# Rounding without relying on the integer cast, in a transformer layer's quantized feed-forward

## The reference, cut to what matters

```
def _quant_weight(w):
    s = jnp.clip(jnp.mean(jnp.abs(w)), EPS, None)
    wq = jnp.clip(jnp.round(w / s), -1.0, 1.0) * s
    ...
def _quant_act(x):
    scale = 127.0 / jnp.clip(jnp.max(jnp.abs(x), axis=-1, keepdims=True), EPS, None)
    xq = jnp.clip(jnp.round(x * scale), -128.0, 127.0) / scale
    ...
def _bitlinear(x, w):
    return jnp.einsum('bsi,oi->bso', _quant_act(x), _quant_weight(w))
...
x = x + attention(layernorm(x))
h = gelu(_bitlinear(layernorm(x), w1))      # 4096 wide
x = x + _bitlinear(h, w2)
```

## Time and profile before

| what | us |
|---|---|
| median of 3 runs | 8665.15 (8665.02 to 8674.39) |
| the profiled execution, timed as the runs are | 8699.92 |
| its span, slowest core | 8698.4 (8636.6 to 8698.4 over the cores) |
| TensorE busy | 4222.9 |
| VectorE busy | 2331.2 |
| ScalarE busy | 1927.1 |

### The profile page before, as it was taken

One profiled execution on the slowest core, in us unless ns is written; L12 is line 12 of the kernel. 1 busy time (PEld: TensorE's weight loads), 2 busy tenths in 40 slices (PEclk: granted clock), 3 DMA queues, 4 the chain that ended last, 5 costly groups with the idle time before them and its releaser, 6 DMA issues.

```text
span 8698.4 us, 58407 instructions; the slowest of 8 cores (8636.6 to 8698.4 us)
## 1 busy us (share of the span) xinstructions
PE 4222.9 (49%) x19456; PEld 1649.1 (19%) x19456; DVE 2331.2 (27%) x4241; ACT 1927.1 (22%) x2129; POOL 0.2 (0%) x4
## 2 busy tenths in 40 slices
PE   4224555666666536546666664203334433035545
PEld 0000211222222212112222222101112211012222
DVE  0431323111111122331111111465444444730000
ACT  1012211444443222014444342111000011001111
POOL 0000000000000000000000000000000000000000
PEclk8666665555555556555555555556666666568778
DMA  4242100000000110000000001111122211221221
GB/s 165 92 135 89 32 0 0 1 1 1 1 1 1 37 63 18 0 0 1 1 1 1 1 1 41 61 44 49 61 85 72 73 58 58 73 85 44 73 78 56
DMA packets 199057, 358.61 MB, mean 41 GB/s; under 512 B 23257, under 2 KB 154718, under 8 KB 194674
## 3 DMA queue, kind: packets, MB, share of 16 engines
q1 hardware_dynamic: 198770, 354.87, 12.6%
HBM read 279.29 MB, written 75.50 MB: 41 GB/s over the span
## 4 chain that ended last, share of the span: by engine, by line
PE 43%; DVE 24%; ACT 15%; issue 8%; DMA 6%; SPq 3%; DVEq 1%; ACTq 0%
ACT pslab L763 7%; PE ps_PV L773 6%; PE ps_S L752 6%; PE ps_F L1182 6%; PE ps_F L1068 5%; PE pss L265 4%; PE ps_qn L730 3%; PE ps_W L830 2%; PE ps_mu L606 2%; DVE colmisc L1099 2%; DVE ao_tm L785 2%; PE ps_rs L610 2%; PE ps_proj L485 2%; PE ps_trH L1121 2%; DMA f2xst<-scr_x 2%
## 5 line engine op out<-in xcount | busy, mean ns | idle before, releaser
L752 PE MATMUL ps_S<-qt,kt 65*128 65x512 bf16 x2048 | 985.1, 611 | 278.9 <-ACT pslab L763 242.6
L763 ACT ACTIVATE pslab<-ps_S 128x1024 bf16<-128x1024 f32 x1024 | 994.6, 1021 | 152.3 <-PE ps_S L752 150.4
L1182 PE MATMUL ps_F<-hqin,w2tb 128*128 128x512 bf16 x2048 | 493.5, 403 | 541.1 <-DMA f2xst<-scr_x 408.9
L773 PE MATMUL ps_PV<-vaug,pslab 128*128 128x65 bf16 x8192 | 531.5, 242 | 457.2 <-DVE ao_tm L785 369.5
L783 DVE RECIPROCAL colmisc<-ps_PV 128x1 f32<-128x1 f32 x512 | 86.1, 168 | 1950.9 <-PE ps_PV L773 1950.9
L773 PEld LDWEIGHTS ps_PV<-vaug,pslab 128*128 128x128 bf16 x8192 | 463.2, 129 | 573.0 <-issue 573.0
L265 PE MATMUL pss<-wab,s_onescolf 128*1 128x512 f32 x512 | 309.4, 755 | 518.9 <-ACT wab L245 306.1
L1068 PE MATMUL ps_F<-w1tb,yi_fm 128*128 128x512 bf16 x2048 | 462.8, 389 | 179.7 <-DMA w1tb<-scr_w1t 179.2
L1121 PE MATMUL ps_trH<-s_idb,hqtm 128*128 128x128 bf16 x1024 | 129.3, 305 | 757.1 <-DVE colmisc L1114 655.0
L1182 PEld LDWEIGHTS ps_F<-hqin,w2tb 128*128 128x128 bf16 x2048 | 211.0, 103 | 802.0 <-issue 597.8
L752 PEld LDWEIGHTS ps_S<-qt,kt 65*128 65x128 bf16 x2048 | 152.5, 108 | 1108.8 <-issue 1108.8
(11 more groups left out here) (174 smaller groups left out, 4041.1 us busy)
## 6 DMA issues: line engine op xcount, KB each, us to landing
w1tb<-scr_w1t SPq DMA_DIRECT2D x512, 128.0 KB, 2.5
wst<-w1t SPq DMA_DIRECT2D x24, 2048.0 KB, 8.4
wst<-w2t SPq DMA_DIRECT2D x96, 512.0 KB, 3.6
xstage<-x SPq DMA_DIRECT2D x64, 512.0 KB, 3.7
scr_hq<-hqfm SPq DMA_DIRECT2D x256, 128.0 KB, 2.0
hqin<-scr_hq SPq DMA_DIRECT2D x256, 128.0 KB
scr_x<-x2asm SPq DMA_DIRECT2D x32, 512.0 KB, 2.9
f_xst<-scr_x SPq DMA_DIRECT2D x32, 512.0 KB, 3.2
```

The costliest lines, as they stand in the source:

```text
L752: ins = q.matmul(out=psS[kt % 2][:, 512 * s:512 * (s + 1)], lhsT=kt65[:, N * g + 128 * kt: N * g + 128 * (kt + 1)], rhs=qt65[hb][:, 1024 * ...
L763: sA.inc(q.activation(out=pslab[:, 1024 * kt:1024 * (kt + 1)], in_=psS[kt % 2][:], func=AF.Exp))
L773: ins = q.matmul(out=psPV[:], lhsT=pslab[:, 1024 * kc + 128 * qt: 1024 * kc + 128 * (qt + 1)], rhs=vaug[:, 1040 * g + 65 * kc: 1040 * g + ...
L1182: ins = q.matmul(out=psF[:, half:half + 512], lhsT=w2tb[:, 1024 * hc + 128 * dc: 1024 * hc + 128 * (dc + 1)], rhs=hqin[:, 512 * hc:512 * ( ...
```

## The change

The casts to int32 no longer do the rounding by themselves.
- w_tern: the two casts and the clamp (three passes) become two comparisons, with 0.5 and with -0.5, and the subtraction of their results (three passes). The integer buffer wint goes.
- ln3_quant_phase and ffn1_phase: 128 is added in the scaling pass; the cast to int32 is cast back to f32, subtracted from the value, the remainder compared with 0.5 and the outcome added to the whole number (`is_gt` and `add` in one pass over two tensors), and 128 taken off again while writing bf16. Two passes over 1024 columns become five. ffn1 gets an f32 buffer hflt of 1024 columns.

```diff
--- before.py
+++ after.py
@@ -311,7 +311,6 @@
         wst = st.enter_context(nc.sbuf_tensor(_u("wst2"), [128, 2 * cols], F32))
         wtmp = st.enter_context(nc.sbuf_tensor(_u("wtmp"), [128, cols], F32))
         werr = st.enter_context(nc.sbuf_tensor(_u("werr"), [128, cols], F32))
-        wint = st.enter_context(nc.sbuf_tensor(_u("wint"), [128, cols], I32))
         if scr is not None:
             wtb = st.enter_context(nc.sbuf_tensor(_u("wtb"), [128, 2 * cols], BF16))
         bia, bib, boa, bob, bv = dIa.n, dIb.n, dOa.n, dOb.n, sV.n
@@ -349,10 +348,11 @@
                                              in1=src, op0=OP.mult, op1=OP.add))
                 VS(q, q.scalar_tensor_tensor(out=wtmp[:], in0=werr[:], scalar=rscol[:, 0:1],
                                              in1=wtmp[:], op0=OP.mult, op1=OP.add))
-                VS(q, q.tensor_copy(out=wint[:], in_=wtmp[:]))
-                VS(q, q.tensor_copy(out=wtmp[:], in_=wint[:]))
-                sV.inc(q.tensor_scalar(out=dst, in0=wtmp[:], scalar1=1.0, scalar2=-1.0,
-                                       op0=OP.min, op1=OP.max))
+                VS(q, q.tensor_scalar(out=werr[:], in0=wtmp[:], scalar1=0.5, scalar2=None,
+                                      op0=OP.is_gt))
+                VS(q, q.tensor_scalar(out=wtmp[:], in0=wtmp[:], scalar1=-0.5, scalar2=None,
+                                      op0=OP.is_lt))
+                sV.inc(q.tensor_tensor(out=dst, in0=werr[:], in1=wtmp[:], op=OP.subtract))
         barrier()
         st.close()
 
@@ -1004,9 +1004,15 @@
                                       in1=colmisc[:, 5:6], op=OP.mult))
                 sV.inc(q.tensor_copy(out=colmisc[:, 15:16], in_=colmisc[:, 7:8]))
                 VS(q, q.tensor_scalar(out=ytmp[:], in0=ytmp[:], scalar1=colmisc[:, 7:8],
-                                      scalar2=None, op0=OP.mult))
+                                      scalar2=128.0, op0=OP.mult, op1=OP.add))
                 VS(q, q.tensor_copy(out=yint[:], in_=ytmp[:]))
-                sV.inc(q.tensor_copy(out=yib[:, D * (t % 2):D * (t % 2 + 1)], in_=yint[:]))
+                VS(q, q.tensor_copy(out=yjunk[:, 0:D], in_=yint[:]))
+                VS(q, q.tensor_tensor(out=ytmp[:], in0=ytmp[:], in1=yjunk[:, 0:D],
+                                      op=OP.subtract))
+                VS(q, q.scalar_tensor_tensor(out=ytmp[:], in0=ytmp[:], scalar=0.5,
+                                             in1=yjunk[:, 0:D], op0=OP.is_gt, op1=OP.add))
+                sV.inc(q.tensor_scalar(out=yib[:, D * (t % 2):D * (t % 2 + 1)], in0=ytmp[:],
+                                       scalar1=128.0, scalar2=None, op0=OP.subtract))
                 q.wait_ge(sP.h, bp + t + 1)
                 ins = q.tensor_copy(out=yir[:, :, 128 * t:128 * (t + 1)],
                                     in_=pstr[:, 1024 * (t % 2):1024 * (t % 2 + 1)]
@@ -1037,6 +1043,7 @@
         htile = st.enter_context(nc.sbuf_tensor(_u("htile"), [128, 4 * HID], F32))
         hqtm = st.enter_context(nc.sbuf_tensor(_u("hqtm"), [128, HID], BF16))
         hint = st.enter_context(nc.sbuf_tensor(_u("hint"), [128, 1024], I32))
+        hflt = st.enter_context(nc.sbuf_tensor(_u("hflt"), [128, 1024], F32))
         hqfm = st.enter_context(nc.sbuf_tensor(_u("hqfm"), [128, NC_H * 512], BF16))
         hqr = hqfm[:].rearrange("p (c w) -> p c w", w=512)
         for bl in range(8):
@@ -1107,10 +1114,16 @@
                     VS(q, q.tensor_scalar(out=colmisc[:, 7:8], in0=colmisc[:, 7:8],
                                           scalar1=127.0, scalar2=None, op0=OP.mult))
                     VS(q, q.tensor_scalar(out=ht, in0=ht, scalar1=colmisc[:, 7:8],
-                                          scalar2=None, op0=OP.mult))
+                                          scalar2=128.0, op0=OP.mult, op1=OP.add))
                     for sl in range(4):
-                        VS(q, q.tensor_copy(out=hint[:], in_=ht[:, 1024 * sl:1024 * (sl + 1)]))
-                        VS(q, q.tensor_copy(out=hqtm[:, 1024 * sl:1024 * (sl + 1)], in_=hint[:]))
+                        hs = ht[:, 1024 * sl:1024 * (sl + 1)]
+                        VS(q, q.tensor_copy(out=hint[:], in_=hs))
+                        VS(q, q.tensor_copy(out=hflt[:], in_=hint[:]))
+                        VS(q, q.tensor_tensor(out=hs, in0=hs, in1=hflt[:], op=OP.subtract))
+                        VS(q, q.scalar_tensor_tensor(out=hs, in0=hs, scalar=0.5,
+                                                     in1=hflt[:], op0=OP.is_gt, op1=OP.add))
+                        VS(q, q.tensor_scalar(out=hqtm[:, 1024 * sl:1024 * (sl + 1)], in0=hs,
+                                              scalar1=128.0, scalar2=None, op0=OP.subtract))
                     sV.inc(q.tensor_copy(out=colmisc[:, 15:16], in_=colmisc[:, 7:8]))
                 for rnd in range(4):
                     @blk.tensor
```

## The result

The changed kernel takes 9240.9 us (median of 8 runs, 9226.0 to 9255.5), the kernel before on the same chip 8665.1 (8 runs, 8651.5 to 8674.4). The ratio is 1.0664, its 95% interval 1.0652 to 1.0676: 576 us more, 565 to 586. The forecast was 9252, that is 586.5 more. The profiled execution took 9247.8 us, that of the kernel before 8699.9.

The account below looks back on a forecast made before the run. It took VectorE's work in the four edited places, with other engines waiting, to bound the kernel. Added passes of 442.0, 110.5, 17.0 and 17.0 us sum to 586.5, on a median of 8665.2: 9252 us, range 9225 to 9325.

Parts of the forecast that it names:

- The prices: VectorE passes at 1024 columns: 694 ns for one tensor in, 1225 for two; 0.103 us between dependent operations.
- the lower end: Comparisons in w_tern cost 694 ns at 1024 columns, like other one-tensor passes; this gave the 586.5 us sum.
- rival 1: Comparisons in w_tern run at the slow two-tensor rate: 68 us more, 9320 us; chance 0.06.
- rival 2: The two-tensor passes run at the fast rate, 694 ns at 1024 columns: 9047 us; chance 0.02.
- ffn1: Three added passes in each of 128 slices, 3.453 us a slice, nothing covering them: 442.0 us.
- ln3: The same three added passes once per tile, 32 times 3.453 us, nothing covering them: 110.5 us.
- w_tern on w2: Subtraction at the two-tensor price, 32 rows of 1024 columns, not covered by loads: 17.0 us.
- on w1: w_tern at 4096 columns, 8 rows; each load queued behind the previous row's store, so no cover: 17.0 us.
- rival 3: In ffn1 longer TensorE idle keeps 8 matmul bursts longer at the low clock: 16 us, 9268; chance 0.04.
- Cover: In ffn1 TensorE or ScalarE works on the next tile during VectorE's rounding, hiding the added passes: 8665 us; chance 0.02.

Follow-up runs that it names:

- the two kernels with the early Gelu: In ffn1 Gelu waits only for the block's last product, not the previous tile's copies: on the changed kernel 9129.9 us, on the kernel before 8540.4.
- after_sp: The changed kernel with SP issuing the load of row r+1 ahead of the store of row r in w_tern: 9190.3 us, ratio 1.0589.
- after_pipe: The changed kernel with ffn1 reordered, TensorE transposing slice n while VectorE rounds slice n+1: 9103.1 us, ratio 1.0491.

## Why the prediction was right

- *What bounds the stages.* That VectorE's work in the four places is on the chain, with 27% of busy time over the whole, held: the parts alone add up, and the two kernels with the early Gelu differ by the same 459 us.
- *The prices.* Every new pass came out within 1 ns of the price taken for it, the comparisons at the lower end, so rival 1 (9320) fell; two-tensor passes at 1225, so rival 2 (9047) fell. VectorE's busy time, forecast at about 2868 us, is 2867.8. Here the trace agrees with the Trainium skill (VectorE: DVE Perf Modes, What auto-detection actually checks): the comparison with a constant takes 694 ns, as the clamp in its place did (L354), although the arithmetic is another.
- *ffn1* 442.0 forecast, 442.1 measured alone; *ln3* 110.5 and 111.4; *w_tern on w2* 17.0 and 18.1 alone; *on w1* 17.0 and 16.0 to 19.7. That the store ahead of the load in SP's queue, and not the load itself, makes w1's wait was shown by after_sp.
- *TensorE's clock.* A burst of the changed kernel's ffn1, the columns as in the earlier trace rows:

```profile
7266.00:7270.00 4.00, 3.71 (x10) 1.36 (x11) 0.14 (x1) 0.00 (x0) 0.00 (x0) 0.56 0.66 210
7270.00:7325.00 55.00, 53.30 (x247) 23.83 (x245) 23.86 (x32) 0.76 (x1) 0.00 (x0) 1.00 0.37 116
```

  The first 4 us had 0.56 in the mean and the rest 1.00, much as in the earlier trace rows. All eight bursts show the same: in the 20 us ahead of each the clock was 0.50 in both kernels, in the first 4 us it was 0.50 to 0.66 before and 0.50 to 0.62 after, and a burst took 58.5 us in the mean before and 58.7 after. A longer wait took nothing from bursts that start low anyway, and ffn2 kept its 993 us. The conclusion of rival 3 holds, though the row taken for it does not show it: the 0.52 in the earlier trace rows is of the stretch behind the burst, not ahead of it.
- *Cover.* None: over the 32 waits, one a tile, TensorE waited for 13.9 us more each in the mean.
- *The difference of the medians*, 576, is 11 below the forecast's 586.5, which lies just above the interval's upper end (586). That may be chance. The difference of the two profiled executions, 548, is 39 below, and can be placed: on the two slowest cores the three stretches with edits are 590.4 longer together, and what is missing is in attention, whose code is the same: 4690.9 us before, 4636.5 after. Of these 54 us, 49 are TensorE's busy time (2754.7 and 2705.7 us in that stage); this is also why its busy time over the whole fell by 48.6, where the forecast had it unchanged. The slowest core of before lay on the half of the chip with the lower clock (last section). On cores 0 to 3, whose projections differ by at most 8 us between the two profiles, the median of the spans grew by 586.1. So the terms of the forecast stand to some us each; that this one figure meets 586.5 to under 1 us is luck, as the stages scatter by more.

## What to carry to other kernels

Read from the chain and the waits whether an engine's work has anything beside it; where it has none, count passes by the price of their form (sources, pointer scalars, columns) and add the sum to the time, whatever the engine's share. Of the three ways of rounding that ran here the cheapest is the one folded into passes that run anyway: a constant added in the scaling and taken off in the write costs one pass, two casts cost two, a cast and its repair five. Before one calls a wait for a load "room", look at what stands ahead of that load in its queue.

## What the runs showed of the hardware that was not expected

Attention, whose code no kernel touched, makes most of the scatter: it takes 4609.3 to 4690.9 us over the 16 cores of the two profiles. The same 35 us of one execution, the profile of before, in the first projections (L485) on core 3 and on core 4:

```profile
1010.00:1045.00 35.00, 35.00 (x164) 15.85 (x162) 0.00 (x0) 12.19 (x21) 0.00 (x0) 1.00 0.00 0
1010.00:1045.00 35.00, 34.82 (x132) 14.51 (x134) 0.00 (x0) 9.38 (x16) 0.00 (x0) 0.81 0.00 0
```

Cores 0 to 3 all had a granted clock of 1.00 there, cores 4 to 7 all 0.81, and in the same time 132 to 135 matmuls stand against 161 to 164. Over both sequences the three groups of projections (L485, L492, L499) were busy 172 to 174 us on cores 0 to 3 and 202 to 207 us on cores 4 to 7. In the profile of the changed kernel all eight cores had 1.00 in that part of the code (1025 to 1060 us); in its second sequence (3380 to 3390 us) cores 0 and 1 had 0.81 and the other six 1.00. So the lower clock is found with and without the edit, on several cores of one die at once and not always the same. On the two slowest cores the 256 matmuls of the query projection of the first sequence took 67.4 us before and 58.3 after, and all projections were busy 29 us longer before, of the 54 us by which attention differed. What brings the lower clock about, no run here shows.

A VectorE pass that waits for its predecessor's semaphore starts 0.80 us after it, the same pass without the wait 0.61 us, at 1024 columns of the 694 ns form (after and after_pipe). A wait between two passes thus costs 0.19 us, although both follow each other on one engine.
